# Seven half products in place of eight for pairs of token tiles in the down projection of a ternary feed-forward layer

## The reference, cut to what matters

```
h = hidden_states + attention(layernorm(hidden_states))
xq = round(127 * ln / max|ln|)                 # ln = layernorm(h), per token, -127..127
gate = silu(xq . sign(w_gate).T * scales)      # weights are -1, 0, 1 times one mean
up   = xq . sign(w_up).T * scales
mid  = gate * up                               # 4096 per token
mq   = round(127 * mid / max|mid|)             # per token, -127..127
y    = h + (mq . sign(w_down).T) * scales      # 4096 -> 1024
```

## Time and profile before

| what | value |
|---|---|
| three runs | 1127.58, 1137.93 and 1185.99 us |
| median | 1137.93 us |
| the profiled execution: its own time | 1130.37 us |
| its span on the slowest core (core 3) | 1128.8 us |
| PE busy, share of the span | 94% |
| DVE, ACT, POOL busy | 55%, 44%, 18% |
| down products on the chain that ended last (L649) | 19% of the span |

### The profile page before, as it was taken

The page is one execution under the profiler, slowest core; times in us unless marked ns, Lnnn a source line. Parts: engine busy times, 40 slices in busy tenths (PEclk is TensorE's granted clock), DMA queues, the critical chain, the costliest instruction groups (busy, mean ns, idle before and its releaser), DMA issues.

```text
span 1128.8 us, 13492 instructions; the slowest of 8 cores (1110.0 to 1128.8 us)
## 1 busy us (share of the span) xinstructions
PE 1066.1 (94%) x5414; PEld 500.2 (44%) x5414; DVE 621.8 (55%) x1133; ACT 499.1 (44%) x603; POOL 207.1 (18%) x132
## 2 busy tenths in 40 slices
PE   5898879999999989989699999999999999999998
PEld 2344435544444444434244444444444444444443
DVE  4526745566576577856444744744744744744311
ACT  3535767877888837555422222222222222222110
POOL 0000002023433500465221021021021021011010
PEclk9999999999999999999889999999999999999999
DMA  8997997799989955699951351351341351231240
GB/s 273 294 309 235 335 323 260 254 335 297 318 265 321 308 171 157 119 221 248 150 122 41 81 121 40 83 121 44 79 121 42 80 121 43 70 94 43 52 112 38
DMA packets 201502, 190.22 MB, mean 169 GB/s; under 512 B 169824, under 2 KB 173920, under 8 KB 194016
## 3 DMA queue, kind: packets, MB, share of 16 engines
q1 hardware_dynamic: 179584, 162.10, 52.4%
q10 hardware_dynamic: 21856, 27.27, 8.6%
HBM read 139.01 MB, written 29.36 MB: 149 GB/s over the span
## 4 chain that ended last, share of the span: by engine, by line
PE 67%; DMA 11%; ACT 9%; DVE 8%; POOL 2%; issue 2%; ACTq 0%; SPq 0%; DVEq 0%; POOLq 0%
PE ps L669 33%; PE ps L649 19%; PE ps L486 11%; DMA wst<-wdT 4%; DMA wst<-wuT 4%; ACT ek L1242 2%; POOL wst L402 2%; DVE nm L872 2%; DVE lg L868 2%; ACT wg L430 1%; ACT wd L430 1%; PE ps L516 1%; ACT wst L416 1%; ACT wu L430 1%; DMA wst<-wgT 1%
## 5 line engine op out<-in xcount | busy, mean ns | idle before, releaser
L669 PE MATMUL ps<-wg,aqT 128*128 128x512 fp8e4 x1024 | 244.2, 382 | 8.6 <-ACT silu L1316 6.6
L669 PE MATMUL ps<-wu,aqT 128*128 128x512 fp8e4 x1024 | 242.6, 380 | 0.1
L1316 ACT ACTIVATE silu<-ps,l 128x512 f32<-128x512 f32 x128 | 87.6, 685 | 311.1 <-PE ps L669 301.3
L1183 DVE SCALAR_TENSOR_TENSOR hmid<-ps,l,silu 128x512 f32<-128x512 f32 x128 | 95.8, 748 | 142.8 <-PE ps L669 100.2
L669 PEld LDWEIGHTS ps<-wu,aqT 128*128 128x128 bf16 x1024 | 100.2, 98 | 122.3 <-issue 1.1
L669 PEld LDWEIGHTS ps<-wg,aqT 128*128 128x128 bf16 x1024 | 98.5, 98 | 122.0 <-ACT silu L1316 8.5
L1362 POOL TENSOR_SCALAR hmid<-hmid,hsc 128x1024 f32<-128x1024 f32 x64 | 72.6, 1153 | 305.3 <-DVE hsc L1204 242.0
L486 PE MATMUL ps<-wck,xT 128*128 128x512 bf16 x512 | 117.2, 383 | 8.9 <-ACT vst L1259 8.9
L402 POOL TENSOR_SCALAR wst<-wst,msum 128x2048 f32<-128x2048 f32 x42 | 84.6, 2018 | 182.2 <-DMA wst<-wuT 85.1
L1175 DVE SCALAR_TENSOR_TENSOR xr<-ps,hsc,xr 128x512 f32<-128x512 f32 x32 | 24.0, 751 | 170.3 <-PE ps L649 170.3
L486 PE MATMUL ps<-wv,xT 128*128 128x512 bf16 x448 | 102.8, 383 | 0.0
(11 more groups left out here) (109 smaller groups left out, 1095.2 us busy)
## 6 DMA issues: line engine op xcount, KB each, us to landing
wst<-wuT SPq DMA_DIRECT2D x26, 1024.0 KB, 14.2
wst<-wgT SPq DMA_DIRECT2D x26, 1024.0 KB, 10.2
xr<-x_own SPq DMA_DIRECT2D x32, 512.0 KB, 8.2
wst<-wdT ACTq DMA_DIRECT2D x16, 1024.0 KB, 11.6
s_hq<-hqs SPq DMA_DIRECT2D x32, 512.0 KB, 4.1
wst<-wdT SPq DMA_DIRECT2D x13, 1024.0 KB, 9.5
xr<-x_oth SPq DMA_DIRECT2D x16, 512.0 KB, 13.0
y<-xr SPq DMA_DIRECT2D x16, 512.0 KB, 3.3
```

What stands on the lines that cost most here:

```text
L669: pe(lambda e, c=c: e.matmul(out, a[:, c * 128:c * 128 + 128], w8[:, c * DI + 512 * oc:c * DI + 512 * oc + 512], start=(c == 0), stop=(c = ...
L1183: dv(lambda e: e.scalar_tensor_tensor(hmid[:, 512 * oc:512 * oc + 512], U[oc % 2], l2[:, s + 6:s + 7], sl, op0=ALU.mult, op1=ALU.mult), [a ...
L1316: ac(lambda e: e.activation(silu[:, (oc % 2) * 512:(oc % 2) * 512 + 512], G[oc % 2], ACTF.Silu, bias=0.0, scale=l2[:, s + 5:s + 6]), [at(" ...
```

## The change

From the third pair on (tiles 4 and 5, up to 14 and 15), the down products of two tiles a = 2p and b = 2p + 1 are made together. Their quantized mids are cut into two halves of 2048 inner values, and the weight into four quarters of 2048 x 512. Eight half products of 16 matmuls each become seven (Strassen's scheme), whose operands are sums of halves and sums of quarters. All sums are small integers, so they are exact in bf16 and in fp8. Each product is then added to, or taken from, one or two of the four pieces of the result (512 columns of a or of b).

- PE: `pe_m` does 16 matmuls, for the products in the order 3, 5, 4, 2, 1, 7, 6. They use KB[1] and KB[2] in turn, and each waits until the last update from the bank's product before is done.
- DVE: `dv_yp` makes twelve updates of 128x512 per pair where `dv_y` made four. `dv_e` makes five sums e1 to e5 of transposed halves in place, each in two instructions of 128x1024 in bf16. Product 5 waits for e1, 2 for e2, 1 for e3, 7 for e4 and 6 for e5. `dv_dsc` makes two small scales a tile where there was one.
- Weight sums: five, each in eight instructions of 128x1024 in fp8 (`w_sum`). Three are on DVE, one instruction after every slice of stages 4, 5 and 6. Two are on POOL, four instructions in each of stages 4 to 7, behind `gp_xb` in its list.
- Places: stage 3 does the down product of tile 0, stage 4 that of tile 1, stage 5 those of tiles 2 and 3. Then stages 6, 8, 10 and 12 end with products 3, 5, 4, 2 of a pair, stages 7, 9, 11 and 13 with its 1, 7, 6. Stage 14 ends with 3, 5 and stage 15 with 4, 2, 1, 7, 6. The seven of the last pair come after stage 15.
- `load_hq` and `store_y` wait for the product, or the update, that now comes last.

```
+PAIR0 = 2
+    MORD = (3, 5, 4, 2, 1, 7, 6)
+    M_L = {1: (0, 0), 2: (1, 0), 3: (0, 0), 4: (1, 1), 5: (0, 1), 6: (1, 0),
+           7: (0, 1)}
+    M_E = {1: 3, 2: 2, 3: None, 4: None, 5: 1, 6: 5, 7: 4}
+    M_C = {1: [(0, 0, 1), (1, 1, 1)], 2: [(1, 0, 1), (1, 1, -1)],
+           3: [(0, 1, 1), (1, 1, 1)], 4: [(0, 0, 1), (1, 0, 1)],
+           5: [(0, 0, -1), (0, 1, 1)], 6: [(1, 1, 1)], 7: [(0, 0, 1)]}
...
+    def down_at(t):
+        if t == TQ:
+            return [("P", TQ // 2 - 1, MORD)]
+        if t < 2 * PAIR0 + 2:
+            return [("D", k) for k in
+                    {3: (0,), 4: (1,), 5: (2, 3)}.get(t, ())]
+        p = t // 2 - 1
+        n = 4 if t < TQ - 2 else 2
+        return [("P", p, MORD[n:] if t % 2 else MORD[:n])]
...
+    def pe_m(p, m):
+        k = m_no[0] % 2
...
+        ts = (2 * p, 2 * p + 1) if m in (4, 2, 1, 7, 6) else (2 * p,)
+        after = [m_free[k]] + [at("hqT", t, h) for t in ts for h in range(2)]
+        after.append(at(*M_W[m]) if p == PAIR0 and M_W[m] else None)
+        after.append(at("e", p, M_E[m], 1) if M_E[m] else None)
+        for c in range(16):
+            pe(lambda e, c=c: e.matmul(
+                KB[1 + k], l_[:, c * 128:c * 128 + 128], M_R[m][:, c, :],
+                start=(c == 0), stop=(c == 15)),
+               after if c == 0 else (), ("M", p, m) if c == 15 else None)
...
+    def dv_yp(p, m):
+        for a, h, sg in M_C[m]:
...
+            dv(lambda e, x2=x2, k=k: e.scalar_tensor_tensor(
+                x2, m_bank[p, m], hsc[:, k:k + 1], x2, op0=ALU.mult,
+                op1=ALU.add),
...
+    def dv_e(p, k):
+        a, b = 2 * p, 2 * p + 1
+        o, i, op, after = {
+            1: ((a, 1), (a, 0), ALU.add, []),
+            2: ((b, 0), (b, 1), ALU.add, []),
+            3: ((a, 0), (b, 1), ALU.add, [at("M", p, 3)]),
+            4: ((a, 1), (a, 0), ALU.subtract, [at("M", p, 5)]),
+            5: ((b, 0), (a, 0), ALU.subtract, [at("M", p, 2)])}[k]
...
+        for n in range(2):
+            o_ = hqT_half(*o)[:, D * n:D * n + D]
+            i_ = hqT_half(*i)[:, D * n:D * n + D]
+            dv(lambda e, o_=o_, i_=i_: e.tensor_tensor(o_, o_, i_, op=op),
+               after, ("e", p, k, n))
...
+    def w_sum(put, k, j):
...
+        put(lambda e: e.tensor_tensor(o[:, sl, :], x[:, sl, :], y[:, sl, :],
+                                      op=op, saturate=False), after,
+            ("ws", k, j))
+    def dv_downs(t):
...
+                if m == MORD[0]:
+                    for k in (2 * p, 2 * p + 1):
+                        dv_dsc(k)
+                    dv_e(p, 1)
+                dv_yp(p, m)
+                if m == 3:
+                    dv_e(p, 2)
+                    dv_e(p, 3)
+                if m == 5:
+                    dv_e(p, 4)
+                if m == 2:
+                    dv_e(p, 5)
...
+    for k, t in ((1, 4), (2, 5), (3, 6)):
+        for j in range(8):
+            ws_dve[t, j] = [(k, j)]
...
+    ws_pool = {4: [(0, j) for j in range(4)], 5: [(0, j) for j in range(4, 8)],
+               6: [(4, j) for j in range(4)], 7: [(4, j) for j in range(4, 8)]}
```

More of the change, by code:

```diff
@@ L202, in build_nc @@
     junk = sb("junk", 2048, F8, rJK)
+    wsm = sb("wsm", 3 * 8192, F8, rWS)
     xr2 = sb("xr2", 2 * D, F32, rWS + 8192 * (NWST - 1))
@@ L211, in hqT_at, with hqT_half, wd_q, wsum @@
         return b, c * 128
+    def hqT_half(t, k):
+        b, o = hqT_at(t, 16 * k)
+        return b[:, o:o + 2048]
+    def wd_q(r, c):
+        return wd8[:, r * 16 * D:(r + 1) * 16 * D].rearrange(
+            "p (j i) -> p j i", i=D)[:, :, 512 * c:512 * c + 512]
+    def wsum(k):
+        return wsm[:, k * 8192:(k + 1) * 8192].rearrange(
+            "p (j i) -> p j i", i=512)
+    MORD = (3, 5, 4, 2, 1, 7, 6)
+    M_L = {1: (0, 0), 2: (1, 0), 3: (0, 0), 4: (1, 1), 5: (0, 1), 6: (1, 0),
+           7: (0, 1)}
+    M_R = {1: wsum(0), 2: wd_q(0, 0), 3: wsum(1), 4: wsum(2), 5: wd_q(1, 1),
+           6: wd_q(0, 1), 7: wd_q(1, 0)}
+    M_W = {1: ("ws", 0, 7), 2: None, 3: ("ws", 1, 7), 4: ("ws", 2, 7),
+           5: None, 6: ("ws", 3, 7), 7: ("ws", 4, 7)}
+    M_E = {1: 3, 2: 2, 3: None, 4: None, 5: 1, 6: 5, 7: 4}
+    M_C = {1: [(0, 0, 1), (1, 1, 1)], 2: [(1, 0, 1), (1, 1, -1)],
+           3: [(0, 1, 1), (1, 1, 1)], 4: [(0, 0, 1), (1, 0, 1)],
+           5: [(0, 0, -1), (0, 1, 1)], 6: [(1, 1, 1)], 7: [(0, 0, 1)]}
+    M_LAST = {}
+    for m in MORD:
+        for a, h, _ in M_C[m]:
+            M_LAST[a, h] = m
+    def y_done(t, h):
+        if t < 2 * PAIR0:
+            return at("y", t, h)
+        return at("yp", t // 2, M_LAST[t % 2, h], t % 2, h)
+    def hqT_free(t):
+        if t < 2 * PAIR0:
+            return at("down", t, 1)
+        return at("M", t // 2, MORD[-1])
+    def down_at(t):
[7 more added lines that the diff above has]
+        return [("P", p, MORD[n:] if t % 2 else MORD[:n])]
     def xf(t, a=0, b=D):
@@ L655, in pe_down, with pe_downs @@
                ("down", t, h) if c == 31 else None)
+    m_free = [at("y", 2 * PAIR0 - 1, 0), at("y", 2 * PAIR0 - 1, 1)]
+    m_bank, m_no = {}, [0]
+    def pe_m(p, m):
+        k = m_no[0] % 2
+        m_no[0] += 1
+        m_bank[p, m] = KB[1 + k]
+        a, r = M_L[m]
+        l_ = hqT_half(2 * p + a, r)
+        ts = (2 * p, 2 * p + 1) if m in (4, 2, 1, 7, 6) else (2 * p,)
[7 more added lines that the diff above has]
+               after if c == 0 else (), ("M", p, m) if c == 15 else None)
+        a, h, _ = M_C[m][-1]
+        m_free[k] = at("yp", p, m, a, h)
+    def pe_downs(t):
+        for d in down_at(t):
+            if d[0] == "D":
+                pe_down(d[1], 0)
+                pe_down(d[1], 1)
+            else:
+                for m in d[2]:
+                    pe_m(d[1], m)
     for p in range(3):
@@ L704, in build_nc @@
                 pe_at(t + 1)
[L705 to L710, removed]
+        pe_downs(t)
+    pe_downs(TQ)
     def load_x(i):
@@ L780, in store_y @@
         sp(f"dY{t % NXF}", y_out.ap()[t * 128:(t + 1) * 128, :], xf(t),
-           [at("y", t, 0), at("y", t, 1)], ("yst", t))
+           [y_done(t, 0), y_done(t, 1)], ("yst", t))
     def hq_out(t):
@@ L804, in load_hq @@
         spt(f"dG{h}", b[:, o:o + 2048], r,
-            [at("hst", t, h), at("down", t - 3, 1) if t >= 3 else None,
+            [at("hst", t, h), hqT_free(t - 3) if t >= 3 else None,
              at("Q", TQ - 1), at("EQ", TQ - 2)] +
@@ new lines, in build_nc @@
+    y_prev = {}
+    def dv_e(p, k):
[6 more added lines that the diff above has]
+            5: ((b, 0), (a, 0), ALU.subtract, [at("M", p, 2)])}[k]
+        after = after + [at("hqT", t, h) for t in {o[0], i[0]}
+                         for h in range(2)]
+        after += {3: [at("e", p, 1, 1)], 4: [at("e", p, 3, 1)],
+                  5: [at("e", p, 3, 1), at("e", p, 2, 1)]}.get(k, [])
+        for n in range(2):
[3 more added lines that the diff above has]
+               after, ("e", p, k, n))
@@ new lines, in w_sum @@
+    def w_sum(put, k, j):
+        o, x, y, op = [
+            (wsum(0), wd_q(0, 0), wd_q(1, 1), ALU.add),
+            (wsum(1), wd_q(0, 1), wd_q(1, 1), ALU.subtract),
+            (wsum(2), wd_q(1, 0), wd_q(0, 0), ALU.subtract),
+            (wd_q(0, 1), wd_q(0, 1), wd_q(0, 0), ALU.add),
+            (wd_q(1, 0), wd_q(1, 0), wd_q(1, 1), ALU.add)][k]
+        sl = slice(2 * j, 2 * j + 2)
+        after = [at("unit", len(units) - 1)]
+        if k > 2:
+            after += [at("down", 2 * PAIR0 - 1, 1),
+                      at("ws", (1, 2)[k - 3], 7)]
+        put(lambda e: e.tensor_tensor(o[:, sl, :], x[:, sl, :], y[:, sl, :],
+                                      op=op, saturate=False), after,
+            ("ws", k, j))
@@ new lines, in dv_downs @@
+    def dv_downs(t):
+        for d in down_at(t):
+            if d[0] == "D":
+                dv_y(d[1], 0)
+                dv_y(d[1], 1)
+                continue
+            p = d[1]
+            for m in d[2]:
+                if m == MORD[0]:
[10 more added lines that the diff above has]
+                    dv_e(p, 5)
@@ L1169, in dv_y @@
         if h == 0:
[L1170 to L1174, removed]
+            dv_dsc(t)
         dv(lambda e: e.scalar_tensor_tensor(
@@ L1205, in dv_hscale @@
            [at("hc", t)], ("hs", t))
+    ws_dve = {}
+    for k, t in ((1, 4), (2, 5), (3, 6)):
+        for j in range(8):
+            ws_dve[t, j] = [(k, j)]
     for t in range(TQ):
@@ L1230, in build_nc @@
                     dv_aqt(t + 1)
+            for k, j in ws_dve.get((t, oc), ()):
+                w_sum(dv, k, j)
         dv_hscale(t)
[L1232 to L1237, removed]
+        dv_downs(t)
+    dv_downs(TQ)
     def ac_ek(i):
@@ L1376, in build_nc @@
             gp_xb(t + 2)
+        for k, j in ws_pool.get(t, ()):
+            w_sum(gp, k, j)
         for n in ffn_units.get(t, {}).values():
```

16 lines of the change are left out of this document (added).

## The result

The changed kernel took 1142.9 us (median of 16 runs, 1133.7 to 1148.4) against 1132.9 for the kernel before (16 runs). The ratio is 1.0073, with a 95% interval of 1.0045 to 1.0100: 0.7% slower, or 8.3 us, although TensorE does 96 matmuls less. The ratio leaves out executions in which the chip was in a slower state, so it is not quite the ratio of the two medians. The prediction said 1140 us, or +9.8 us.

What follows compares the result with a forecast made beforehand. PE was taken as the bound, without idle time from stage 4 on. Matmuls -20.7, weight sums +11.8, product 5 +17.4 and clock +1.3 gave +9.8 us on 1130.4, so 1140 us, range 1119 to 1152.

Steps and rivals of the forecast that it cites:

- The count: PE, six pairs with 16 matmuls less each: 96 x 0.216 = 20.7 us saved, the most the change can win.
- The weight sums, predicted 11.8 us: Stages 4 to 6: DVE's sums and POOL's delay PE, 3.6 us in stages 4 and 5 each, 4.6 in stage 6.
- DVE's own length: Stages 4 to 6: four DVE sums before the scale make PE wait 1.6 us in each, were DVE alone.
- the meetings: DVE two-input instructions wait for POOL's running one: 0 to 2.35 us each, 1.0 taken, 2.0 for two per stage.
- rival (C): The square root's tiny DVE instructions wait for POOL too, 4.7 us more in stages 4 and 5 each: 1149 us, chance 0.15.
- (A): The forecast as summed, with DVE's full list and waits for POOL: 1140 us, 1134 to 1147, chance 0.40.
- Product 5, predicted 11.4 + 6.0 us: PE waits for e1 behind the stage's end in DVE's list: 2.85 us four times, 6.0 in stage 6.
- The bf16 price: Each of e1's two DVE instructions was taken at 0.65 us, with 1.22 as the longer end for the range.
- The clock, predicted 1.3 us: Stage 6: its 6.0 us idle time of PE lowers the clock and costs 1.3 us more; nothing added elsewhere.
- rows 9: Profile rows: eight matmuls took 3.19 us after 3.31 us of PE idle time, 1.90 after 2.02.
- The cover that the prediction called thin: Last pair: tile 15's load lands 6.6 us later at most, products 3 and 5 take 6.9, so nothing lost.
- Rival (D): POOL keeps its turn, so e1 starts only after the fourth rounding: +26 us, 1156 us, up to 1178, chance 0.08.

Runs made afterwards that it cites:

- Run 8: Kernel with e1 earlier, DVE's weight sums moved late and POOL's behind the square root, changed by spreading DVE's sums further: 1115.4 us, ratio 0.9842.
- run 3: Changed kernel with POOL's 16 weight sums left out, so not the layer's result: PE from stage 4 on takes 545.1 us (median).
- run 5: Changed kernel with POOL's weight sums of a stage held until that stage's square root is done: ratio 0.9973 to the kernel before.
- run 1: Changed kernel with e1 made after slice 5 of even stages 6 to 14, last pair unchanged: ratio 1.0018 to the kernel before.
- run 2: Changed kernel with DVE's weight sums moved beside the down products and into late slices and slice 1 of stage 7: ratio 1.0002.

## Why the prediction was right

**The count.** 2673 matmuls became 2577 in this stretch, 20.7 us less. Run 8 shows it whole: 528.3 us on the best core.

**The weight sums, predicted 11.8 us.** Measured on core 6: idle 5.0 and 4.4 us in stages 4 and 5, and 2.6 in stage 6 ahead of product 5, or 12.0; on all cores 11.9 to 13.6, median 12.8. The sum was right, its parts less so. Stages 4 and 5 were put at 3.6 us each and stage 6 at 4.6, so too little in the one made up for too much in the other. In stages 4 and 5, 1.6 were put down to DVE's own length, where run 3 has mostly 0.8 to 1.3, and 2.0 to the meetings, where POOL's sums add 3 us and more to what run 3 has. In stage 6 POOL's four sums start with the stage, as predicted, but on core 6 they are over 8.5 us into it and meet only two residual adds of DVE (1.32 and 1.54 us long), no weight sum:

```profile
699.26 8.21 POOL L1313 TENSOR_TENSOR wd<-wd 128x1024 fp8e4<-128x1024 fp8e4 x4 [0.38 <-PE ps L707]
```

```profile
704.29 1.32 DVE L1162 TENSOR_TENSOR xr<-xr,tmp 128x384 f32<-128x384 f32 x1
...
706.34 1.54 DVE L1162 TENSOR_TENSOR xr<-xr,tmp 128x384 f32<-128x384 f32 x1
```

The prediction looked at U6 and the transposes; on core 6 PE also waited before U5, 1.1 us by the rows, in stages 4 and 5. The DVE timeline of stage 4, then POOL's and PE's, shows the meetings (start, us, what, [idle before]):

```profile
602.59 2.59 DVE L1196 TENSOR_SCALAR tmp<-xr,mv 128x1024 f32<-128x1024 f32 x1
605.10 3.02 DVE L1313 TENSOR_TENSOR wsm<-wd 128x1024 fp8e4<-128x1024 fp8e4 x1
...
610.51 1.45 DVE L1177 SCALAR_TENSOR_TENSOR nw<-l,nw 128x1 f32<-128x1 f32 x1
...
613.54 1.22 DVE L1313 TENSOR_TENSOR wsm<-wd 128x1024 fp8e4<-128x1024 fp8e4 x1
```

```profile
602.63 9.32 POOL L1313 TENSOR_TENSOR wsm<-wd 128x1024 fp8e4<-128x1024 fp8e4 x4
```

```profile
608.84 1.90 PE L757 MATMUL ps<-wu,aqT 128*128 128x512 fp8e4 x8 [1.08 <-DVE hmid L1350]
...
615.48 2.85 PE L757 MATMUL ps<-wu,aqT 128*128 128x512 fp8e4 x8 [3.01 <-DVE hmid L1350]
618.48 1.03 PE L697 MATMUL ps<-identh,aq 128*128 128x128 f16 x8 [0.15 <-ACT aq L1227]
```

While POOL's four sums run, the centred row takes 2.59 us where its shortest was 0.75 and its median 1.76, and the weight sum behind it 3.02 where 1.22 is the sum alone, as taken. A third meeting, 1.2 us, falls on the square root's first two-input instruction. That was rival (C), which the prediction gave 0.15. Its mechanism is shown (runs 3 and 5). In stage 4 three cores have one such wait, three have two and two have none; in stage 5 seven cores have two, and only core 6 has one. Two look like this (DVE, stage 5 of core 3):

```profile
631.57 1.46 DVE L1177 SCALAR_TENSOR_TENSOR nw<-l,nw 128x1 f32<-128x1 f32 x1
...
633.25 1.74 DVE L1183 TENSOR_TENSOR l<-l,nw 128x1 f32<-128x1 f32 x1
```

Alone they take 0.22 and 0.16, so the two waits are 2.8 us, against the 4.7 that (C) priced for two POOL sums. So part of what (A) got right in size came by the mechanism of (C).

**Product 5, predicted 11.4 + 6.0 us.** The step was right: e1 in DVE's list behind the end of the stage holds it (run 1). Its size was too large: 1.8 us four times and 4.1 once, 11.4. The bf16 price was right (two instructions of 0.68). What failed is the order of turns: the prediction let one of POOL's roundings run between e1's two halves. The rows of stage 8, DVE and then POOL:

```profile
818.77 1.97 DVE L1295 TENSOR_TENSOR hqTa<-hqTa 128x1024 bf16<-128x1024 bf16 x2
```

```profile
818.48 6.31 POOL L1533 TENSOR_SCALAR hmid<-hmid,hsc 128x1024 f32<-128x1024 f32 x4 [16.26 <-DVE hsc L1371]
```

The first half waited for the first rounding, 0.7 us, and the second followed it at once: 1.97 us for both. POOL's four took 6.31 in place of 4.4 (two take 2.21), so it is POOL that waited after that.

**The clock, predicted 1.3 us.** This was the term that was too small. It is what remains of a core's time from stage 4 on when 528.0 and the idle time are taken off: 3.0 to 7.5 us, median 5.5 (on core 6: 554.4 - 528.0 - 23.4 = 3.0). The mean granted clock of its stages 4 and 5 is 0.96 and 0.97, so for a part of them the lower level, 1.2 GHz, was granted. From stage 4 on that was so for 6.8 to 17.1 us by core; half of that, 3.4 to 8.5 us, is what half the clock can cost. The prediction looked for an idle time like that of rows 9 in stage 6 only, though its own 3.6 us in stages 4 and 5 would have been longer than the 3.31 of those rows, had they come in one piece. On core 6 stage 4 has two idle times, 1.08 and 3.01 us, with 3.6 us of matmuls between them, and the eight matmuls behind the second took 2.85 in place of 1.89.

Its stage 6, where the prediction had the price, paid none (clock 1.00); on the other seven cores the clock of stage 6 is 0.93 to 0.97. Runs 1 and 2 bear the term out as one of its own: their idle time is the same (medians 16.7 and 16.9 us), the rest is 4.5 us in run 1, which keeps stages 4 and 5 as they were, and 0.5 in run 2. The idle times of 1.8 us in stages 8 to 14 cost no clock on any core. The length of the last idle time alone doesn't decide it. In the first row, of stage 4 of the changed kernel on core 4 (granted clock 1.00), 2.89 us leave the next eight matmuls at 1.90. In the second, of stage 6 of run 2 on core 5 (0.96), the sixteen matmuls behind 2.00 us take 5.31 in place of 3.6:

```profile
602.00 1.90 PE L757 MATMUL ps<-wu,aqT 128*128 128x512 fp8e4 x8 [2.89 <-DVE hmid L1350]
```

```profile
692.67 5.31 PE L729 MATMUL ps<-wd,hqTb 128*128 128x512 fp8e4 x16 [2.00 <-DVE hqTb L1295]
```

What else decides it stays open here.

**The sum.** With the medians of the cores, -20.7 + 12.8 + 11.4 + 5.5 = +9.0 us, against +9.8 predicted, +9.1 by the traces and +8.3 by the ratio; on core 6, -20.7 + 12.0 + 11.4 + 3.0 = +5.7, which is 554.4 less 548.7. Two terms were off, product 5 by 6 us too much and the clock by 4 too little, and they made up for each other, as the parts of the weight sums did. So the forecast's steps were right (DVE's list before the scale, the meetings with POOL, e1 behind the end of the stage), and its closeness is in good part luck. Two slips in it changed nothing: the first piece of rows 2 is sixteen matmuls, not two; and the price of 1.22 for a sum in bf16 adds, by the prediction's own terms, 5 x (1.14 + 0.5) = 8.2 us, not 10.

**The rest.** The cover that the prediction called thin was thin indeed. Stage 15 and the last pair took 69.07 us for their 320 matmuls, with no idle time, on three cores of the eight. On the others they took up to 1.2 us more. On two of these product 4 waited 0.6 and 0.8 us for the load of tile 15, which the prediction had named as a sign of being wrong; it is too small to change the sum. Stage 7 had no idle time on six cores, and 0.8 and 1.1 us on two, where 0 to 1 was said. Rival (D) did not come: DVE was let in at every rounding.

## What to carry to other kernels

Ask of every instruction that is added to an engine's list where PE stands at that moment, and not how busy the engine is on average: DVE was 55% busy and had 2.2 us of slack in the first half of a stage, and the same sums cost next to nothing when they were put where it had slack, most of them beside the down products. An operand's preparation that stands behind the end of a stage costs what its chain takes beyond the work that PE still has (5.1 us, less 3.45 of product 3); moved two slices ahead it was free in stages 8 to 14. And when DVE and POOL both have work that reads SBUF, let POOL's wait for the last of the DVE instructions that it holds up: that move alone took 8 us of idle time away.

## What the hardware showed that was not expected

- A DVE instruction on one value per partition waited 1.2 us for POOL's instruction of 2.0 us (1.452 against 0.220 us), and the next of its kind 1.6 (1.74 against 0.16). With POOL's sums left out or moved it never did. This is what the Trainium skill, page SBUF — State Buffer, section "SBUF: two separate sides", says of any instruction with two SBUF inputs, and the traces of runs 3 and 5 agree.
- Of two DVE instructions back to back, the second went ahead of a POOL instruction that had been waiting since before the first had ended (1.97 us for both of e1's halves, 6.31 for four roundings that take 4.4 alone).
- Sums of 128x1024: in bf16, in place, 0.68 us on DVE; in fp8 1.22 on DVE and 2.0 on POOL, where the f32 add takes 2.35.
- Idle time of PE cost more than itself: on top of 24.5 us of it (median of the cores) 5.5 us came from the clock. In run 2 it was 0.5 us on top of 16.9, and in the changed kernel the 1.8 us waits of stages 8 to 14 cost nothing more.
